# Self-attention values of four chunks in one TensorE visit, in five units of eight

## What is computed

```
x = x + xattn(layernorm(x), ctx)      # 32 query heads, 8 key/value heads of 128, rope, causal, then Wd
x = x + attn(layernorm(x))            # 32 heads of 16, biases on q, k, v, o, causal over 64 tokens
x = x + ffn(layernorm(x))             # base projection + 8 experts of rank 16, gated by a threshold
```

## Time and profile before

| what | value |
|---|---|
| median of 3 runs | 706.79 us (705.87 to 707.06) |
| the profiled execution | 706.06 us, span 704.2 us |
| granted clock of TensorE over the span | 1.00 of full |
| PE busy | 694.8 us, 99% |
| PE weight loads | 564.0 us, 80% |
| DVE busy | 516.4 us, 73% |
| ACT busy | 373.0 us, 53% |
| POOL busy | 471.6 us, 67% |

### The profile page before, as it was taken

The page is one execution under the profiler, slowest core; times in us unless marked ns, Lnnn a source line. Parts: engine busy times, 40 slices in busy tenths (PEclk is TensorE's granted clock), DMA queues, the critical chain, the costliest instruction groups (busy, mean ns, idle before and its releaser), DMA issues.

```text
span 704.2 us, 12879 instructions
## 1 busy us (share of the span) xinstructions
PE 694.8 (99%) x4841; PEld 564.0 (80%) x4841; DVE 516.4 (73%) x815; ACT 373.0 (53%) x560; POOL 471.6 (67%) x360
## 2 busy tenths in 40 slices
PE   8999999899999999999999999999999999999998
PEld 6887888688888888888888888887888888887886
DVE  5566988967767767857758758748668888899734
ACT  6356665634743743753653653654246777665220
POOL 2698155877777778778777877844525799985630
PEclk9999999999999999999999999999999999999999
DMA  7645613140400311310310312200300101011003
GB/s 263 221 150 176 172 46 106 75 164 17 135 31 18 132 35 38 106 45 30 104 45 30 104 45 65 87 16 2 104 2 1 46 31 33 2 47 46 16 1 119
DMA packets 25736, 51.08 MB, mean 73 GB/s; under 512 B 2400, under 2 KB 10720, under 8 KB 25696
## 3 DMA queue, kind: packets, MB, share of 16 engines
q1 hardware_dynamic: 25696, 50.53, 21.8%
HBM read 40.04 MB, written 10.49 MB: 72 GB/s over the span
## 4 chain that ended last, share of the span: by engine, by line
PE 83%; DVE 5%; POOL 4%; DMA 3%; issue 2%; ACT 2%; SPq 1%; DVEq 0%; POOLq 0%; ACTq 0%
PE pj L1625 12%; PE pv L1712 10%; PE pj L1712 10%; PE pj L1816 9%; PE tp L1625 8%; PE sc L1681 4%; PE tp L1712 4%; PE pj L2000 3%; PE pv L1611 3%; PE sc L1866 2%; PE tp L1879 2%; PE pv L1890 2%; PE pv L1699 2%; PE tp L1688 2%; PE sc L1699 2%
## 5 line engine op out<-in xcount | busy, mean ns | idle before, releaser
L496 POOL TENSOR_TENSOR sw<-sw,cst 128x512 f32<-128x512 f32 x72 | 96.9, 1345 | 42.3 <-ACT sw L681 42.0
L520 POOL TENSOR_TENSOR sm<-sm,mx 128x512 f32<-128x512 f32 x64 | 73.0, 1147 | 29.6 <-DVE mx L1234 16.0
L525 POOL TENSOR_TENSOR sm<-sm,rz 128x512 f32<-128x512 f32 x64 | 70.7, 1120 | 27.0 <-DVE rz L1249 27.0
L502 POOL TENSOR_TENSOR qr<-t,sw 128x512 f32<-128x512 f32 x54 | 73.9, 1369 | 7.7
L1625 PE MATMUL tp<-x,w 128*128 128x512 f32 x288 | 74.5, 395 | 0.0
L805 ACT ACTIVATE sm<-sm 128x512 f32<-128x512 f32 x64 | 40.1, 633 | 53.4 <-POOL sm L520 53.1
L514 POOL TENSOR_TENSOR w<-raw,w 128x896 fp32r<-128x896 f32 x24 | 50.3, 2118 | 26.0 <-ACT w L658 26.0
L1816 PE MATMUL pj<-xh,ws 128*128 128x512 f32 x192 | 64.6, 402 | 0.2 <-ACT kb L899 0.2
L1625 PEld LDWEIGHTS tp<-x,w 128*128 128x128 f32 x288 | 53.0, 188 | 10.8
L658 ACT ACTIVATE w<-raw 128x1792 fp32r<-128x1792 f32 x15 | 25.6, 1705 | 59.7 <-DVE raw L1109 59.7
L1625 PE MATMUL pj<-xt,w 128*128 128x512 f32 x192 | 51.7, 407 | 0.0
(11 more groups left out here) (279 smaller groups left out, 1849.6 us busy)
## 6 DMA issues: line engine op xcount, KB each, us to landing
rawd<-in_w_d SPq DMA_DIRECT2D x16, 512.0 KB, 3.4
raw<-in_w_q SPq DMA_DIRECT2D x15, 512.0 KB, 3.3
kscr<-sm SPq DMA_DIRECT2D x16, 256.0 KB, 2.1
vscr<-sm SPq DMA_DIRECT2D x16, 256.0 KB, 2.6
kr<-kscr SPq DMA_DIRECT2D x8, 512.0 KB, 3.2
vv<-vscr SPq DMA_DIRECT2D x16, 256.0 KB, 3.5
raw<-in_w_v SPq DMA_DIRECT2D x4, 512.0 KB, 3.9
X<-in_x SPq DMA_DIRECT2D x4, 512.0 KB, 6.8
```

The source lines that it names most:

```text
L496: pool.tensor_tensor(bs(sw[par][:, :]), bs(sw[par][:, :]), rep(cst[:, C_SIN:C_SIN + S], HB), ALU.mult).then_inc(sin_done, 1)
L502: pool.tensor_tensor(o, bs(t1[par][:, :]), bs(sw[par][:, :]), ALU.add).then_inc(rope, 1)
L520: pool.tensor_tensor(s3, s3, per_group(mx[:, c, :], 8), ALU.subtract).then_inc(subbed, 1)
L525: pool.tensor_tensor(s3, s3, per_group(rz[:, c, :], 8), ALU.mult).then_inc(normed, 1)
```

## The change

The values of a unit's four chunks are computed in one visit at c = 2, in units 0 to 4 (GROUPED = 5); units 5, 6 and 7 keep pairs. pv now holds chunk n in bank n % 2 at columns 0 to 255 (c = 0, 1) or 256 to 511 (c = 2, 3), in all units. pts has four buffers, and pt_copy waits for the values that used the buffer before. DVE's selections of a grouped unit come half at its own c = 2 step (chunks 4v, 4v+1) and half at the next unit's c = 0 step (chunks 4v+2, 4v+3), after the masks; step 10 (v = 5, c = 0) has four of them, 18 and 19 and then its own 20 and 21. In grouped units from v = 1 on the visit waits once, for `ssel >= 4v`; from unit 5 on pv_s(n) waits for `ssel >= n - 1` as before. out_hi(v-1) moves from c = 1 to c = 2, and split_out(v-1) from c = 2 to c = 3, for v = 1 to 5; units 6 and 7 keep both.

```diff
-        pts = [sb(ss, f"pts{i}", [P, 512]) for i in range(2)]
+        pts = [sb(ss, f"pts{i}", [P, 512]) for i in range(SCH)]
...
+        GROUPED = NSU - 3
+
+        def spv_cols(n):
+            return pv[:, n % 2, n % SCH // 2 * 256:n % SCH // 2 * 256 + 256]
...
-                if v and c == (0 if v == NSU - 2 else 2):
+                if v and c == (0 if v == NSU - 2 else 2 if v == NSU - 1 else 3):
                     split_out(v - 1)
...
             def pt_copy(n):
                 act.wait_ge(pt_t, n + 1)
-                act.activation(pts[n % 2][:, :], tp[:, n % 2, :], ACT.Copy).then_inc(pt_done, 1)
+                if SCH <= n <= SCH * GROUPED:
+                    act.wait_ge(spv, n // SCH * SCH)
+                elif n > SCH * GROUPED:
+                    act.wait_ge(spv, n - 3)
+                act.activation(pts[n % SCH][:, :], tp[:, n % 2, :], ACT.Copy).then_inc(pt_done, 1)
...
-                if c == 1 and v and v != NSU - 2:
+                if c == 1 and v == NSU - 1:
+                    out_hi(v - 1)
+                if c == 2 and 0 < v <= GROUPED:
                     out_hi(v - 1)
...
-                src = pv[:, n % 2, 0:256].rearrange("p (b r q) -> p b r q", b=2, r=2)
-                dve.wait_ge(spv, n + 1)
+                src = spv_cols(n).rearrange("p (b r q) -> p b r q", b=2, r=2)
+
+                dve.wait_ge(spv, SCH * v + SCH if v < GROUPED else n + 1)
...
-                for n in pair:
-                    select_out(n)
+
+                if v <= GROUPED and c == 0 and v:
+                    select_out(2 * m - 2)
+                    select_out(2 * m - 1)
+                if v >= GROUPED:
+                    for n in pair:
+                        select_out(n)
+                elif c == 2:
+                    select_out(2 * m - 2)
+                    select_out(2 * m - 1)
...
                 pe.wait_ge(pt_done, n + 1)
-                if n >= 2:
+                if v < GROUPED:
+                    if c == 0 and v:
+                        pe.wait_ge(ssel, n)
+                else:
                     pe.wait_ge(ssel, n - 1)
                 for b in range(2):
                     for t in range(2):
-                        last = pe.matmul(pv[64 * t:64 * t + 64, n % 2, b * P:(b + 1) * P],
+                        last = pe.matmul(spv_cols(n)[64 * t:64 * t + 64, b * P:(b + 1) * P],
                                          vc[h][:, 2 * c + b, t, :],
-                                         pts[n % 2][:, (2 * t + b) * P:(2 * t + b + 1) * P], start=True, stop=True)
+                                         pts[n % SCH][:, (2 * t + b) * P:(2 * t + b + 1) * P], start=True, stop=True)
...
-                pv_s(n)
-                pv_s(n + 1)
+                if v >= GROUPED:
+                    pv_s(n)
+                    pv_s(n + 1)
+                elif c == 2:
+                    for i in range(n - 2, n + 2):
+                        pv_s(i)
```

## The result

The changed kernel takes 713.41 us (median of 4, 712.79 to 714.45) against 706.33 (704.56 to 707.06) before: ratio 1.0111, interval 1.0097 to 1.0125, slower by 7.1 us. The profiled execution took 713.63 us, its span is 711.5; before they were 706.06 and 704.2.

A forecast was written before the change was run, and what follows sets the result against it. It took PE, 99% busy, to bound the kernel. +0.87 - 0.60 + 3.9 + 1.9 = +6.1 us on the profiled 706.06 gave 712.1, put at 712.4 for the median; range 710.0 to 714.8.

The forecast's parts named there:

- the clock: PE's clock behind the wait in step 10: no term in the sum; a fall was priced only in rival (b).
- rival (b): PE stands about 3.6 us in step 10 and its clock falls to half, adding 1.5 to 1.8: 714.1 us; chance 0.10.
- Visits: Each visit to the values left out saves PE 0.15 us; units 1 to 4 together give -0.60 us.
- Unit 0: Step 0 gains nothing, as step 1's transposes already wait for POOL's normalisation; step 1 pays for the moved values: +0.87 us.
- Step 10: PE's first pair of values waits for DVE's selection of chunk 18, now behind two masks and maxima: +3.9 us.
- POOL: Normalisations come late for PE as split_out moves behind the subtractions: 0.55, about 1.2 and 0.2 in units 2 to 4, +1.9 us.

The follow-up runs named there:

- unit0_pairs: The changed kernel with unit 0's values by pairs and its selections in its own steps; 713.08 us, ratio 1.0101 to the kernel before.
- fill_gap: The changed kernel with 30 unused identity transposes on PE in step 10, between the scores and the values; 711.66 us, ratio 1.0076 to before.
- split_only: The kernel before with only POOL's split_out of units 1 to 5 moved from c = 2 to c = 3; 708.39 us, ratio 1.0037.
- sel_first: The changed kernel with DVE's selections of chunks 18 and 19 ahead of the two masks in step 10; 709.29 us, ratio 1.0050 to before.
- best_front: The changed kernel with unit 0 by pairs, split_out at c = 2, selections of chunks 18 and 19 before step 10's sums; 706.29 us, ratio 1.0003 to before.

## Why the prediction was right

The forecast was +6.1 us on the profiled execution and 712.4 for the median; measured are +7.6 (706.06 to 713.63) and 713.41. The sum of the steps holds but for one term, the clock, which it had at nothing. What happened is rival (b), the forecast's own chain with a fall of the clock on top: the measured time lies between the 712.4 of the forecast, at 0.61, and the 714.1 of (b), at 0.10. That 712.4 came so near is in part luck, as the sum at the end of this section shows. The terms:

- *Visits.* 0.15 each; measured 0.13 to 0.14. The 0.44 us between sets of transposes stands in no line of the earlier trace rows; it is from 527.39 to this one:

```profile
527.83 0.60 PE L1557 MATMUL tp<-cst,t 128*128 128x128 f32 x4
```

- *Unit 0.* +0.87 as forecast; unit0_pairs takes it back.
- *Step 10.* 3.9 forecast; 4.0 by fill_gap. The tenth is the time from DVE's end to PE's start, 0.15 in place of the 0.08 I took.
- *POOL.* 1.9 forecast for units 2 to 4; before the visits' gain, measured are about 0.77, 1.23 and 0.13, 2.1. The mechanism I gave was half right. I had put it down to PE asking 1 us earlier *and* split_out coming later; split_only shows that the later split_out alone costs 3.2 us in the order of before, and that it reaches PE also through late_lo and the copies of v. In the changed kernel unit 5 and unit 6 show nothing of it (split_only loses 1.8 us in steps 11 to 13: 8.62, 6.08, 7.80): PE's gap in step 10 gave the other engines the time. With the gap gone, in sel_first, 0.7 of it came out in steps 12 and 13; why not all 1.8 isn't shown. One reading was off by a little: I took PE's starts from the chain, where they are 0.07 later than in the timeline (565.88 against 565.81) that the starts of POOL and DVE come from.
- *The clock.* The missing term, 2.1 us by fill_gap; rival (b) had priced it at 1.5 to 1.8. Its price came from the opening matmuls, read as running at half clock. The trace of before doesn't show that; it gives the full level there, and why these products take 0.41 us each stays open (columns as above):

```profile
0.00:5.00 5.00, 3.57 (x9) 2.64 (x9) 0.69 (x1) 2.22 (x3) 0.88 (x6) 1.00 0.60 191
```

A stretch of 512-column products at a granted 0.50 is in the profiled execution of best_front, and it also answers my evidence against (b), the wait of 1.20 us at 139.10 that left the clock full. There the half level was granted behind waits of 0.35 and 1.06 us at the opening; what brought it no run isolates:

```profile
6.67 1.37 PE L1623 MATMUL pj<-cxh,wk 128*128 128x512 f32 x4 [0.35 <-ACT cxh L664]
9.10 1.14 PE L1623 MATMUL pj<-cxh,wk 128*128 128x512 f32 x2 [1.06 <-ACT cxh L664]
10.04 1.91 PE L1623 MATMUL pj<-cxl,wk 128*128 128x512 f32 x4
```

```profile
9.40:12.60 3.20, 3.20 (x9) 2.44 (x8) 1.61 (x3) 1.92 (x3) 0.87 (x1) 0.50 1.06 391
```

Four products take 1.70 us from 10.04 to the next one at 11.74, 0.43 each, against 0.23 at the full level. So the longest wait that left the clock full was no bound for a wait three times as long. The Trainium skill, TensorE: Matmul & The Clock Gate, "Part 1: The HAM clock gate", says that idleness brings the half rate back. The trace agrees, with a granted 0.50 from 619.8 on, while PE stood for 3.65 us.

Forecast terms and the clock give 6.1 + 2.1 = 8.2 against 8.55 of the stretch; by this measure the forecast was 2.4 us short. The whole time shows less of the miss for reasons that the forecast knew nothing of: the profiled execution came to the stretch 1.2 us earlier than that of before, and the medians differ by 7.1 only, perhaps since two of the four executions had a mean clock of 0.998, about half of the loss at 0.995.

## What to carry to other kernels

When instructions are regrouped on one engine, go through every count that the moved ones raise and ask who waits for it in the very step they moved to: here two selections of 0.7 us, put behind two masks, held PE for 4 us, and the gain in view was 0.75. A filler on a full engine (split_out on POOL) has a right place, in the gap where that engine waits anyway; moved by one position it cost 3.2 us in a kernel in which nothing else had changed. And price a stand of TensorE of some microseconds as the wait plus what may run at half clock behind it: here 4.0 and 2.1 us.

## What the runs showed of the hardware

- After PE stood for 3.65 us the half level was granted for 6.8 us, from 619.8, in the profiled run; after 2.33 us for 3.4 us, and there it began 1.4 us after PE had gone on. With 30 transposes of work that nobody uses in the gap it did not come, in six executions.
- The half level also stands where no wait is long: behind waits of 0.35 and 1.06 us at the opening, the half level was granted from 9.2 to 12.6 us in one profiled execution (best_front), where that of before, with waits of 0.35 us at most, kept the full level.
- At the half level products of 512 columns follow each other by 0.43 us, at the full level by 0.23.
- A visit to the values costs 0.14 to 0.15 us beyond its products, and there is no such break between one pair's values and the next: 16 products in one visit take 1.89 us (start of the values to start of the transposes), two visits of 8 take 2.04.
